# Causal attention in ten steps a group: two narrow key tiles share a step

## The chip, the cores and the metric

The kernel runs on one core of a Trainium2 chip. Inside the core five engines work from instruction queues of their own: TensorE (PE in the rows, with its weight loads as PEld), VectorE (DVE), ScalarE (ACT), GpSimd (POOL) and SyncE (SP, which only issues DMAs here). Each engine runs its instructions in the order in which they are written, and they meet at semaphores. The metric is the device time of one launch in microseconds; lower is better.

## The reference

A layer norm, latent attention with 16 heads over 8 sequences of 1024 tokens, a residual, then a second layer norm and an FP4 feed-forward block. The part that the change touches is the attention proper:

```python
scores = jnp.einsum('bhqd,bhkd->bhqk', Q, K)          # Q, K: 32 plain + 16 rotary features a head
scores = jnp.clip(scores, -80.0, 80.0)
causal = jnp.tril(jnp.ones((S, S), dtype=bool))
scores = jnp.where(causal, scores, -jnp.inf)
weights = jax.nn.softmax(scores / jnp.sqrt(jnp.float32(d_qk)), axis=-1)
attn = jnp.einsum('bhqk,bhkd->bhqd', weights, V)
```

The kernel takes the exponential first and clips afterwards (exp is monotone, so the clip moves to the bounds P_MIN and P_MAX); masked entries become 0 by a bound of 0; the sum over keys (the denominator) is divided out later.

## The kernel before

The program has three stages: projections (until about 350 us), attention (about 350 to 1272 us), feed-forward (to the end). Attention handles 32 **groups**, each one sequence and four heads. Two groups make one turn of a loop: the **even** one (`s == 0`) and the **odd** one (`s == 1`).

Within a group, the 1024 queries are two halves of 512. A **step** is one key tile of 128 keys against the queries of one half that may see it. Half 0 has key tiles 0 to 3, which see 512, 384, 256 and 128 queries; half 1 has key tiles 0 to 7, of which 0 to 4 see 512 queries, and 5, 6, 7 see 384, 256 and 128. So there are NS = 12 steps, numbered k = 0 to 11. A step goes through four operations:

- `score` (PE, L1256): five rounds of matmuls for four heads, keys against queries, into two of three score tiles in PSUM (RING2 = 3; a tile holds two heads).
- `exponentials` (ACT, L1043): two activations, one for each tile (heads 0 and 1, then 2 and 3), from PSUM into one of six `probs` buffers (PROBS = 6; two of the six lie in `r_out`, so the trace shows them as sb_r_out).
- `clip` (DVE, L1121): the 128 columns on the diagonal are clipped against the mask `bound` (L1129), all other columns by L1137. Both take the four heads in one instruction.
- `weigh` (PE, L1276): the probabilities times V, into `ps_o`.

The denominators (`denominators`, L1290) are matmuls with ones into `ps_d`. Eight steps get their own. The four steps k = 4 to 7 (half 1, tiles 0 to 3) are first added up by DVE (`add_up` L1140, four instructions; `add_sums` L1151, two), and one denominator called TOTAL takes their sum.

PE writes, in pass k of its loop: `score` of step k+1, `weigh` of step k-1, then the denominators due. `DENOMS_AT` says at which pass a denominator stands; the last ones of a group and TOTAL (`DENOMS_NEXT`) stand in pass 0 of the next group, behind its `score(1)` and the last `weigh`. ACT and DVE go the same way: in pass k first the exponentials or the clip of step k+1, then what else is due. That is: on ACT the copies of `ps_o` (`copy_out`, between the two exponentials of a step) and of `ps_d` (`copy_denominators`), the rounding of the next group's keys and queries (`round_raw`, L1036, passes 1 and 2), and in the odd group one multiplication for a piece of FP4 weights (L1106, pass 2). On DVE: the low parts of the next group's keys and queries (`rest_of_raw`, L1160), the additions, and small steps of the FP4 quantisation, which are different ones in the even and in the odd group.

Two waits matter below. `score` of a step may begin when the first exponential of the step before has freed its tile:

```python
pe.wait_ge(sc_free, number * 2 + 2)          # L1267
```

And an exponential may write its `probs` buffer when the step that held it before has been weighed and summed (L1049 to L1062).

Of the kernel before, what the change touches and what calls it, by code (L numbers as in the profile page):

```python
# [26 lines left out]
P = 128  # L27
# [6 lines left out]
NI = 4  # L34
# [105 lines left out]
class Front:  # L140


    def __init__(self, nc, ctx, t):
# [16 lines left out]
        self.bound = sb("bound", [P, P])  # L160
# [43 lines left out]
def projections(nc, t, B, front):  # L204
    with ExitStack() as ctx:
# [188 lines left out]
        def _(pool):  # L394
# [19 lines left out]
            pool.affine_select(out=front.bound[:], in_=front.bound[:], compare_op=ALU.is_ge, fill=0.0, base=0,  # L414
                               pattern=[[1, P]], channel_multiplier=-1).then_inc(front.s_cst, 1)
# [287 lines left out]
STEPS = [(half, j, max(0, P * (j - 4 * half))) for half in range(HALF) for j in range(4 * half + 4)]  # L703
NS = len(STEPS)
LOADS2 = 4 * 16


SUMS = [(4, 5), (6, 7)]

TOTAL_STEP = NS - 1  # L710
WARM_UP = 32
# [117 lines left out]
def attention(nc, t, B, front, ahead):  # L829
    with ExitStack() as ctx:  # L830
# [196 lines left out]
        def _(act):  # L1027
# [15 lines left out]
            def exponentials(it2, s, k, first, between=None):  # L1043
                number = step_no(it2, s, k)
                off = STEPS[k][2]
# [3 lines left out]
                act.wait_ge(pv_done, number + 1)  # L1049
# [3 lines left out]
                if k < PROBS and k - PROBS + NS in DENOMS and not first:  # L1053

                    act.wait_ge(denoms_done, denom_no(*preceding(it2, s), DENOMS.index(k - PROBS + NS) + 1))
# [21 lines left out]
            def copy_out(it2, s, half):  # L1077

                act.wait_ge(pv_done, step_no(it2, s, NS if half else 4) + PROBS)
# [7 lines left out]
            def body(it2, s, first, last):  # L1087
                for k in range(NS):
# [3 lines left out]
                    if k == 4:  # L1092
# [14 lines left out]
                    if last and 7 <= k < 7 + GROUPS:  # L1107
                        if k == 7:
                            act.wait_ge(ahead.s_wo, 16)
                        act.copy(ahead.wo_hi[:, k - 7], ahead.x1[:, k - 7]).then_inc(ahead.s_wo_hi, 1)  # L1110
# [7 lines left out]
        def _(dve):  # L1118
            dve.wait_ge(s_cst, 3)

            def clip(it2, s, k):  # L1121
                number = step_no(it2, s, k)
                half, j, off = STEPS[k]

                dve.wait_ge(sc_free, number * 2 + (2 + RING2))
                if j >= 4 * half:

                    pr = probs(k)[:, :, off:off + P]
                    i = dve.scalar_tensor_tensor(out=pr, in0=pr, scalar=P_MIN,  # L1129
                                                 in1=bound[:].unsqueeze(1).to_broadcast([P, NI, P]),  # L1130
# [1044 lines left out]
```

## Time and profile before

| | us |
|---|---|
| median of 3 runs | 2981.09 |
| lowest, highest | 2980.68, 2983.95 |
| the profiled execution, its own time | 2984.09 |
| span of that execution, first to last instruction | 2982.4 |

A row of the timeline gives the start in us from the beginning of the span, the duration, engine, line, operation, output and input, shape, and how many such instructions are merged (x2); square brackets give idle time before it and who ended it. Where two instructions follow one another without a break, their durations overlap a little, and the distance between their starts says what each costs its engine.

### The profile page before, as it was taken

What the parts mean: (1) busy time and instruction counts of PE and PEld (TensorE: products, weight loads), DVE (VectorE), ACT (ScalarE), POOL (GpSimd) and SP (SyncE); (2) the same over time, 40 slices, a digit from 0 to 9 for tenths busy, and PEclk for the clock granted to TensorE, in tenths of its full rate; (3) what the DMA queues carried; (4) which work ended last, traced back from release to release, by engine and by line L of the source; (5) the groups of instructions that cost most, each with busy time, mean ns of one, the idle gap of its engine ahead of it and who ended that gap; (6) DMA issues with size and microseconds to landing.
All of it is one profiled execution on the core that took longest, in us unless ns stands there. A gap on an engine that the chain in (4) does not pass through costs nothing.

```text
span 2982.4 us, 65378 instructions
## 1 busy us (share of the span) xinstructions
PE 2906.9 (97%) x22500; PEld 2133.0 (72%) x22500; DVE 2677.0 (90%) x4593; ACT 1588.7 (53%) x2331; POOL 579.9 (19%) x620
## 2 busy tenths in 40 slices
PE   7999899999999999979999999999999999999999
PEld 6877644444444444468888888888888888888887
DVE  7999788888988988879999999999999999999997
ACT  5666578778777777743333333333333333333333
POOL 3444300000000000012222222222222222222221
PEclk9999999999999999989999999999999999999999
DMA  7889956566565565542222221222222222222220
GB/s 241 283 287 300 290 132 142 135 152 134 138 149 136 138 148 136 140 130 56 59 61 61 60 60 56 53 60 57 60 61 60 60 57 57 55 59 58 60 58 30
DMA packets 335143, 333.27 MB, mean 112 GB/s; under 512 B 60368, under 2 KB 242512, under 8 KB 335056
## 3 DMA queue, kind: packets, MB, share of 16 engines
q1 hardware_dynamic: 335056, 332.26, 40.8%
q8 instruction: 36, 0.59, 0.1%
q14 instruction: 51, 0.42, 0.0%
HBM read 215.52 MB, written 116.65 MB: 111 GB/s over the span
## 4 chain that ended last, share of the span: by engine, by line
PE 55%; DVE 1%; ACT 0%; issue 0%; POOL 0%; DVEq 0%
PE p_ring L2048 20%; PE p_ring L2074 16%; PE ps_od L2048 12%; PE ps_od L2028 6%; PE p_ring L2062 1%; PE ps_od L2074 0%; PE p_ring L2090 0%; PE p_ring L2028 0%; PE p_ring L2055 0%; DVE sb_wg_lo L1936 0%; DVE sb_x_amax L106 0%; DVE sb_stage L1892 0%; POOL sb_stage L1664 0%; DVE sb_xq L120 0%; ACT sb_wg_hi L1753 0%
## 5 line engine op out<-in xcount | busy, mean ns | idle before, releaser
L1065 ACT ACTIVATE sb_probs<-scores 128x1024 f32<-128x1024 f32 (+3 forms) x512 | 405.7, 839 | 112.1 <-PE scores L1271 105.4
L1664 POOL TENSOR_TENSOR sb_stage<-sb_stage,sb_h_inv 128x512 f32<-128x512 f32 (+1 forms) x192 | 190.4, 992 | 857.7 <-DVE sb_h_inv L112 857.7
L2048 PE MATMUL p_ring<-sb_wg_hi,sb_xq_hi 128*128 128x512 f32 (+1 forms) x1024 | 294.9, 369 | 1.8 <-DVE sb_xq_lo L1920 1.1
L2048 PE MATMUL p_ring<-sb_wg_lo,sb_xq_hi 128*128 128x512 f32 (+1 forms) x1024 | 290.6, 365 | 0.0
L2048 PE MATMUL p_ring<-sb_wg_hi,sb_xq_lo 128*128 128x512 f32 (+1 forms) x1024 | 289.4, 364 | 0.0
L2074 PE MATMUL p_ring<-sb_wd_hi,sb_ht_hi 128*128 128x512 f32 x693 | 275.0, 397 | 0.0
L1271 PEld LDWEIGHTS scores<-sb_q_hi,sb_k_hi 32*128 32x128 f32 x1536 | 73.5, 181 | 280.3 <-ACT sb_probs L1065 156.1
L813 POOL TENSOR_TENSOR sb_at_in<-sb_at_in,sb_inv_in 128x512 f32<-128x512 f32 x64 | 95.0, 1485 | 909.1 <-DMA sb_inv_in<-dinv 908.8
L2074 PE MATMUL p_ring<-sb_wd_hi,sb_ht_lo 128*128 128x512 f32 x693 | 270.0, 390 | 0.0
L2074 PE MATMUL p_ring<-sb_wd_lo,sb_ht_hi 128*128 128x512 f32 x693 | 270.0, 390 | 0.0
L1738 ACT ACTIVATE sb_stage<-sb_stage,sb_code_zero 128x512 uint8<-128x512 f32 (+1 forms) x192 | 139.7, 728 | 239.3 <-DVE sb_stage L122 239.3
L1065 ACT ACTIVATE sb_r_out<-scores 128x1024 f32<-128x1024 f32 (+2 forms) x256 | 184.6, 762 | 89.2 <-PE scores L1271 89.2
L1286 PE MATMUL ps_od<-sb_probs,sb_v 128*32 128x512 f32 (+3 forms) x2048 | 225.5, 512 | 0.0
L2048 PEld LDWEIGHTS p_ring<-sb_wg_hi,sb_xq_lo 128*128 128x128 f32 x1024 | 189.1, 188 | 21.8
L2048 PEld LDWEIGHTS p_ring<-sb_wg_lo,sb_xq_hi 128*128 128x128 f32 x1024 | 188.5, 188 | 21.4
L2048 PEld LDWEIGHTS p_ring<-sb_wg_hi,sb_xq_hi 128*128 128x128 f32 x1024 | 185.1, 188 | 22.5 <-issue 2.3
L1137 DVE TENSOR_SCALAR sb_probs<-sb_probs 128x1536 f32<-128x1536 f32 (+3 forms) x224 | 196.6, 877 | 3.9 <-ACT sb_probs L1065 3.9
L1716 ACT ACTIVATE sb_stage<-sb_stage 128x512 f32<-128x512 f32 (+1 forms) x192 | 114.3, 595 | 145.5 <-POOL sb_stage L1664 140.1
L120 DVE SCALAR_TENSOR_TENSOR sb_stage<-sb_stage 128x512 f32<-128x512 f32 (+1 forms) x192 | 184.2, 960 | 6.6
L1271 PE MATMUL scores<-sb_q_hi,sb_k_hi 32*128 32x512 f32 (+3 forms) x1536 | 172.3, 438 | 15.1 <-ACT sb_probs L1065 7.1
L1137 DVE TENSOR_SCALAR sb_r_out<-sb_r_out 128x2048 f32<-128x2048 f32 (+1 forms) x96 | 92.0, 959 | 95.8 <-ACT sb_r_out L1065 95.8
L2048 PE MATMUL ps_od<-sb_wg_hi,sb_xq_hi 128*128 128x512 f32 (+1 forms) x512 | 164.4, 402 | 0.0
(216 smaller groups left out, 7193.9 us busy)
## 6 DMA issues: line engine op xcount, KB each, us to landing
kq<-sb_kq_out SPq DMA_DIRECT2D x32, 1024.0 KB, 7.1
sb_kq_raw<-kq SPq DMA_DIRECT2D x64, 512.0 KB, 7.0
sb_xin<-in_L_attn_x_dram SPq DMA_DIRECT2D x32, 512.0 KB, 7.2
v<-sb_v_out SPq DMA_DIRECT2D x64, 256.0 KB, 6.5
rq<-sb_r_out SPq DMA_DIRECT2D x64, 256.0 KB, 4.5
sb_qr<-rq SPq DMA_DIRECT2D x32, 512.0 KB
sb_kr_hi<-kr SPq DMA_DIRECT2D x32, 512.0 KB
sb_kr_lo<-kr SPq DMA_DIRECT2D x32, 512.0 KB
```

Of the source, the lines that this page charges most:

```text
L120: dve.scalar_tensor_tensor(out=tmp, in0=big, scalar=1.5, in1=y, op0=ALU.max, op1=ALU.add).then_inc(sem, 1)
L813: pool.tensor_tensor(at, at, self.inv_in[:], ALU.mult).then_inc(self.at_divided, 1)
L1065: act.activation(probs(k)[:, 2 * pair:2 * pair + 2, off:BANK], scores[(2 * k + pair) % RING2][:, :, off:BANK], ACT.Exp, scale=SCALE).then_ ...
L1137: i = dve.tensor_scalar(pr, pr, P_MAX, P_MIN, ALU.min, ALU.max)
L1271: mm = pe.matmul(scores[(2 * k + i // 2) % RING2][:, i % 2, off:BANK], key[s][rows, keys], query[s][rows, queries], start=(n == 0), stop=( ...
L1286: mm = pe.matmul(ps_o[rows, off:BANK], v_sb[s][:, j, rows], probs(k)[:, i, off:BANK], start=(j == 0), stop=last)
L1664: pool.tensor_tensor(x, x, spread(h_inv[:, a // QB:b // QB], (b - a) // QB), ALU.mult).then_inc(h_y, 1)
L1716: act.mul(h_big[:, h_slot(r, s), 0:b - a], h[:, a:b], MAGIC).then_inc(h_magic, 1)
L1738: act.activation(out, codes, ACT.Identity, bias=code_zero[:], scale=CODE_STEP).then_inc(h_coded, 1)
L2028: i = pe.matmul(ps[:, 0, :], at[a][:, g, :], wo[b][:, g, :], start=(g == 0 and a == b == 0), stop=(g == GROUPS - 1 and a == 1))
L2048: i = pe.matmul(ps[:, m, 0:b0 - a0], xt[a][:, c, :], wg[b][:, m, c, a0:b0], start=(c == 0 and a == b == 0), stop=(c == DC - 1 and a == 1))
L2074: i = pe.matmul(ps[:, 0, :], ht[a][:, c, :], wd[b][:, c, :], start=(c == 0 and a == b == 0), stop=(c == FC - 1 and a == 1))
```

## The change

The key tile that sees 384 queries and the one that sees 128 fill 512 columns together. They now share a step. The 128 queries of the narrow tile lie in columns 0 to 127, the 384 of the other in columns 128 to 511; both diagonals are then in columns 0 to 255, and the mask is written twice, side by side. A half ends with this pair and then the tile that sees 256. NS is 10: steps 0 to 2 are half 0 (512, pair, 256), steps 3 to 9 half 1 (five of 512, pair, 256).

```diff
-STEPS = [(half, j, max(0, P * (j - 4 * half))) for half in range(HALF) for j in range(4 * half + 4)]
+PAIR = ((1, P, P), (3, 3 * P, 0))
+
+
+def parts_of(half):
+
+    whole = [((j, 0, 0),) for j in range(4 * half + 1)]
+    pair = tuple((4 * half + d, off, at) for d, off, at in PAIR)
+    return whole + [pair, ((4 * half + 2, 2 * P, 2 * P),)]
+
+
+STEPS = [(half, parts) for half in range(HALF) for parts in parts_of(half)]
...
-SUMS = [(4, 5), (6, 7)]
+SUMS = [(3, 4), (5, 6)]
...
-DENOMS = [0, 1, 2, 3, 8, 9, 10, 11, TOTAL]
-DENOMS_AT = {3: [0], 4: [1], 5: [2], 6: [3], 9: [8], 11: [9]}
-DENOMS_NEXT = [10, 11, TOTAL]
-DENOMS_HALF = 4
-DENOM_STEP = 6
+DENOMS = [0, 1, 2, 7, 8, 9, TOTAL]
+DENOMS_AT = {3: [0], 4: [1], 5: [2], 8: [7]}
+DENOMS_NEXT = [8, 9, TOTAL]
+DENOMS_HALF = 3
+DENOM_STEP = 5
```

The wait of an exponential for its buffer follows the new numbers: the buffers of steps 0 to 3 were last used by steps 6 to 9 of the group before, four steps back instead of six. Step 6 is one of those that are added up. And a group now takes 20 score tiles, which is no multiple of three, so `score(0)` meets tiles that step 9 of the group before has just used:

```diff
-                act.wait_ge(pv_done, number + 1)
+                earlier = k - PROBS if k >= PROBS else k + PROBS - NS if k + PROBS < NS else k - NS
+                act.wait_ge(pv_done, number + (earlier - k + PROBS + 1))
...
-                    if k - PROBS + NS in x and not first:
+                    if k < PROBS and earlier + NS in x and not first:
...
-                pe.wait_ge(sc_free, number * 2 + 2)
+                pe.wait_ge(sc_free, number * 2 + (3 if k == 0 else 2))
```

On PE, `score`, `weigh` and `denominators` go over the parts of a step, one after the other; matmuls and columns are as many as before. The clip of a pair is two instructions instead of three, the mask clip over 256 columns:

```diff
+                masked = [at for j, q, at in parts if j >= 4 * half]
+                rest = off + P * len(masked)
+                if masked:
+                    pr = probs(k)[:, :, off:rest]
+                    mask = bound[:, 0:rest - off].unsqueeze(1).to_broadcast([P, NI, rest - off])
+                    i = dve.scalar_tensor_tensor(out=pr, in0=pr, scalar=P_MIN, in1=mask, op0=ALU.max, op1=ALU.min)
+                if rest < BANK:
```

What DVE does behind the clips moves to earlier passes; passes 10 and 11 are gone:

```diff
                     elif k == 4:
                         if not last:
                             rest_of_raw(*following(it2, s), 1)
+                        add_up(it2, s, 0, 0, first)
                     elif k == 5:
-                        add_up(it2, s, 0, 0, first)
+                        add_up(it2, s, 0, 1, first)
+                        if s == 1:
+                            own(dve, w_rounded, rounded + 1)
+                            dve.scalar_tensor_tensor(out=w_tmp[:], in0=w_big[:], scalar=1.5, in1=w_sb[:], op0=ALU.max,
+                                                     op1=ALU.add).then_inc(w_rounded, 1)
                     elif k == 6:
-                        add_up(it2, s, 0, 1, first)
+                        add_up(it2, s, 1, 0, first)
                     elif k == 7:
-                        add_up(it2, s, 1, 0, first)
+                        add_up(it2, s, 1, 1, first)
+                        if s == 1:
+                            own(dve, w_rounded, rounded + 2)
+                            dve.scalar_tensor_tensor(out=w_sb[:], in0=w_big[:], scalar=1.5, in1=w_tmp[:], op0=ALU.max,
+                                                     op1=ALU.subtract, reverse1=True).then_inc(w_rounded, 1)
                     elif k == 8:
-                        add_up(it2, s, 1, 1, first)
-                    elif k == 9:
                         add_sums(it2, s, 0)
...
-                    elif k == 10:
+                    elif k == 9:
                         add_sums(it2, s, 1)
```

The last FP4 multiplication of each group (old pass 11) stands behind `add_sums` of pass 9. ACT keeps `round_raw` in passes 1 and 2 and the FP4 multiplication in pass 2; `copy_out` of half 0 goes from pass 4 to pass 3. At the start GpSimd writes the mask twice, and PE runs 36 warm-up matmuls instead of 32. In the last group, ACT's and DVE's rounding of W_O moves forward by two passes.

On DVE, near the end of the odd group (the loop's second group), before:

```order
L1148 TENSOR_TENSOR sb_v_out<-sb_probs 128x1024
L1125 ISA
L1129 SCALAR_TENSOR_TENSOR sb_probs<-sb_probs,sb_bound 128x4x128
L1137 TENSOR_SCALAR sb_probs<-sb_probs 128x4x256
L1148 TENSOR_TENSOR sb_v_out<-sb_probs 128x1024
L1125 ISA
L1129 SCALAR_TENSOR_TENSOR sb_r_out<-sb_r_out,sb_bound 128x4x128
L1137 TENSOR_SCALAR sb_r_out<-sb_r_out 128x4x128
L59 REGISTER_ALU
L1155 TENSOR_TENSOR sb_v_out<-sb_v_out 128x1024
L819 RECIPROCAL sb_chunk<-sb_chunk 128x64
L1125 ISA
```

and of the change, at the same place:

```order
L1151 SCALAR_TENSOR_TENSOR sb_probs<-sb_probs,sb_bound 128x4x256
L1154 TENSOR_SCALAR sb_probs<-sb_probs 128x4x256
L1165 TENSOR_TENSOR sb_v_out<-sb_r_out,sb_probs 128x1024
L59 REGISTER_ALU
L1238 SCALAR_TENSOR_TENSOR sb_piece_y<-sb_piece_big,sb_piece_tmp 128x528
L1144 ISA
L1151 SCALAR_TENSOR_TENSOR sb_probs<-sb_probs,sb_bound 128x4x128
L1154 TENSOR_SCALAR sb_probs<-sb_probs 128x4x128
L59 REGISTER_ALU
L1172 TENSOR_TENSOR sb_v_out<-sb_v_out 128x1024
L837 RECIPROCAL sb_chunk<-sb_chunk 128x64
L1144 ISA
```

The last `add_up` (the second row of L1148 before, L1165 now) now stands behind the clip of the pair, one clip before the group's last instead of two, and the FP4 rounding of L1209 (now L1238) has moved from behind both `add_sums` to in front of both.

On ACT, in passes 1 to 3 of the odd group, before (sb_k_hi0 and sb_q_hi0 are the rounded keys and queries of the next group, sb_piece_big is the FP4 piece):

```order
L1036 CAST sb_k_hi0<-sb_kq_raw 128x1024
L1049 REGISTER_ALU
L1055 REGISTER_ALU
L1064 ISA
L1065 ACTIVATE sb_probs<-scores0 128x2x128
L1064 REGISTER_ALU
L1065 ACTIVATE sb_probs<-scores1 128x2x128
L1036 CAST sb_q_hi0<-sb_kq_raw 128x1024
L1106 ACTIVATE sb_piece_big<-sb_piece_y 128x528
```

and of the change:

```order
L1054 CAST sb_k_hi0<-sb_kq_raw 128x1024
L1074 REGISTER_ALU
L1083 ISA
L1084 ACTIVATE sb_probs<-scores0 128x1024
L1083 REGISTER_ALU
L1084 ACTIVATE sb_probs<-scores1 128x1024
L1054 CAST sb_q_hi0<-sb_kq_raw 128x1024
L1125 ACTIVATE sb_piece_big<-sb_piece_y 128x528
L1083 ISA
L1084 ACTIVATE sb_r_out<-scores2 128x1024
L1098 REGISTER_ALU
L1100 COPY sb_o<-ps_od 128x512
```

Between the two casts the exponentials are now those of a step with 512 columns, where they were those of the step with 128.

## Rows read from the trace of the kernel before

**Rows 1.** Stretch of 300 us in attention: busy us of each engine, clock.

```profile
core 0: us, PE busy (x) PEld busy (x) DVE busy (x) ACT busy (x) POOL busy (x), PEclk, DMA share, GB/s
900.00:1200.00 300.00, 297.61 (x4336) 145.58 (x4337) 259.23 (x327) 236.87 (x327) 0.00 (x0) 1.00 0.60 141
```

**Rows 2.** Timeline of PE: scores of two groups, then an even group's begin.

```profile
672.57 0.45 PE L1271 MATMUL scores<-sb_q_hi,sb_k_hi 32*128 32x384 f32 x4
...
700.84 0.45 PE L1271 MATMUL scores<-sb_q_hi,sb_k_hi 32*128 32x384 f32 x4
...
701.92 0.42 PE L1286 MATMUL ps_od<-sb_r_out,sb_v 128*32 128x128 f32 x8
702.16 0.83 PE L1305 MATMUL ps_od<-sb_r_out,sb_ones 128*32 128x256 f32 x16
702.81 1.04 PE L1305 MATMUL ps_od<-sb_v_out,sb_ones 128*32 128x512 f32 x8
703.78 0.39 PE L1271 MATMUL scores<-sb_q_hi,sb_k_hi 32*128 32x256 f32 x4
...
704.57 1.06 PE L1286 MATMUL ps_od<-sb_probs,sb_v 128*32 128x512 f32 x8
705.57 0.33 PE L1271 MATMUL scores<-sb_q_hi,sb_k_hi 32*128 32x128 f32 x4
705.73 0.28 PE L1271 MATMUL scores<-sb_q_hi,sb_k_lo 32*128 32x128 f32 x4
...
706.28 0.85 PE L1286 MATMUL ps_od<-sb_probs,sb_v 128*32 128x384 f32 x8
707.06 0.50 PE L1271 MATMUL scores<-sb_q_hi,sb_k_hi 32*128 32x512 f32 x4
```

**Rows 3.** Timeline of PE, the same even group, three passes on.

```profile
708.41 0.64 PE L1286 MATMUL ps_od<-sb_probs,sb_v 128*32 128x256 f32 x8
708.87 1.04 PE L1305 MATMUL ps_od<-sb_probs,sb_ones 128*32 128x512 f32 x8
709.84 0.50 PE L1271 MATMUL scores<-sb_q_hi,sb_k_hi 32*128 32x512 f32 x4
...
711.20 0.43 PE L1286 MATMUL ps_od<-sb_probs,sb_v 128*32 128x128 f32 x8
711.44 0.83 PE L1305 MATMUL ps_od<-sb_probs,sb_ones 128*32 128x384 f32 x8
712.39 0.50 PE L1271 MATMUL scores<-sb_q_hi,sb_k_hi 32*128 32x512 f32 x4
```

**Rows 4.** Timeline of ACT: pass 2 of the odd group, pass 4 of the even.

```profile
678.85 1.07 ACT L1036 CAST sb_q_hi<-sb_kq_raw 128x1024 fp32r<-128x1024 f32 x1
679.78 0.67 ACT L1106 ACTIVATE sb_piece_big<-sb_piece_y 128x528 f32<-128x528 f32 x1
680.33 1.96 ACT L1065 ACTIVATE sb_r_out<-scores 128x1024 f32<-128x1024 f32 x2
...
711.31 1.02 ACT L1065 ACTIVATE sb_r_out<-scores 128x1024 f32<-128x1024 f32 x1 [0.85 <-PE scores L1271]
712.24 0.58 ACT L1081 COPY sb_o<-ps_od 128x512 f32<-128x512 f32 x1
712.70 1.04 ACT L1065 ACTIVATE sb_r_out<-scores 128x1024 f32<-128x1024 f32 x1
```

**Rows 5.** Timeline of DVE: the odd group's second half and its end.

```profile
683.46 1.22 DVE L1160 TENSOR_TENSOR sb_k_lo<-sb_kq_raw,sb_k_hi 128x1024 fp32r<-128x1024 f32 x1
684.59 0.43 DVE L1191 TENSOR_SCALAR sb_piece_big<-sb_piece_big 128x528 int32<-128x528 int32 x1
685.50 1.23 DVE L1137 TENSOR_SCALAR sb_r_out<-sb_r_out 128x2048 f32<-128x2048 f32 x1 [0.48 <-ACT sb_r_out L1065]
...
702.10 0.70 DVE L1209 SCALAR_TENSOR_TENSOR sb_piece_y<-sb_piece_big,sb_piece_tmp 128x528 f32<-128x528 f32 x1
702.72 0.68 DVE L1129 SCALAR_TENSOR_TENSOR sb_probs<-sb_probs,sb_bound 128x512 f32<-128x512 f32 x1
703.33 0.95 DVE L1137 TENSOR_SCALAR sb_probs<-sb_probs 128x1536 f32<-128x1536 f32 x1
```

More of the change, by code:

```diff
@@ L1196, in body @@
                                           ALU.max).then_inc(w_scaled, 1)
-                    elif k == 4 and s == 1:
-                        if not last:
-                            rest_of_raw(*following(it2, s), 1)
-                        own(dve, w_rounded, rounded + 1)
-                        dve.scalar_tensor_tensor(out=w_tmp[:], in0=w_big[:], scalar=1.5, in1=w_sb[:], op0=ALU.max,
-                                                 op1=ALU.add).then_inc(w_rounded, 1)
                     elif k == 2 and s == 0:
@@ L1262, in score @@
                     pe.wait_ge(raw_split, it2 * 4 + (s * 2 + 2 + 2))
[L1263 to L1264 removed]
                 rounds = [(k_hi, q_hi), (k_lo, q_hi), (k_hi, q_lo), (kr_hi, qr), (kr_lo, qr)]
[L1267 to L1268 removed]
+                pe.wait_ge(sc_free, number * 2 + (3 if k == 0 else 2))
+                for j, off, at in parts:
+                    keys = slice(j * P, (j + 1) * P)
+                    queries = slice(half * BANK + off, (half + 1) * BANK)
+                    for n, (key, query) in enumerate(rounds):
+                        for i in range(NI):
+                            rows = slice(DH * i, DH * i + DH)
+                            mm = pe.matmul(scores[(2 * k + i // 2) % RING2][:, i % 2, at:at + BANK - off],
+                                           key[s][rows, keys], query[s][rows, queries], start=(n == 0),
+                                           stop=(n == len(rounds) - 1))
+                            if j == parts[-1][0] and n == len(rounds) - 1 and i % 2 == 1:
+                                mm.then_inc(sc_ready, 1)
@@ L1269, in score, with weigh @@
+            def weigh(it2, s, k):
+                number = step_no(it2, s, k)
+                half, parts = STEPS[k]
+                pe.wait_ge(clipped, number + 1)
+                if parts[0][0] == 0:
+                    pe.wait_ge(o_free, half_no(it2, s, half) + 1)
+                last = parts[0][0] == 4 * half + 2
+                for j, off, at in parts:
                     for i in range(NI):
                         rows = slice(DH * i, DH * i + DH)
-                        mm = pe.matmul(scores[(2 * k + i // 2) % RING2][:, i % 2, off:BANK], key[s][rows, keys],
-                                       query[s][rows, queries], start=(n == 0), stop=(n == len(rounds) - 1))
@@ L1273, in score @@
-                        if n == len(rounds) - 1 and i % 2 == 1:
-                            mm.then_inc(sc_ready, 1)
-            def weigh(it2, s, k):
-                number = step_no(it2, s, k)
-                half, j, off = STEPS[k]
-                pe.wait_ge(clipped, number + 1)
-                if j == 0:
-                    pe.wait_ge(o_free, half_no(it2, s, half) + 1)
-                last = j == 4 * half + 3
-                for i in range(NI):
-                    rows = slice(DH * i, DH * i + DH)
-                    mm = pe.matmul(ps_o[rows, off:BANK], v_sb[s][:, j, rows], probs(k)[:, i, off:BANK],
-                                   start=(j == 0), stop=last)
+                        mm = pe.matmul(ps_o[rows, off:BANK], v_sb[s][:, j, rows], probs(k)[:, i, at:at + BANK - off],
+                                       start=(j == 0), stop=last)
@@ L1303, in denominators @@
                     pe.wait_ge(d_free, half_no(it2, s, half) + 1)
-                for i in range(NI):
-                    mm = pe.matmul(ps_d[DH * i:DH * i + DH, off:BANK], ones[:], src[:, i, off:BANK], start=start,
-                                   stop=n in (DENOMS_HALF - 1, len(DENOMS) - 1))
+                for j, off, at in parts:
+                    for i in range(NI):
+                        mm = pe.matmul(ps_d[DH * i:DH * i + DH, off:BANK], ones[:], src[:, i, at:at + BANK - off],
+                                       start=start, stop=n in (DENOMS_HALF - 1, len(DENOMS) - 1))
                 mm.then_inc(denoms_done, 1)
```

79 lines of the change are left out of this document (34 added, 45 removed).

## The prediction

> **What bounds the kernel now.** Look first at the busy times by stretch. In the middle of attention PE is busy 297.6 of 300 us at the full clock (1.00, its 2.4 GHz level), DVE 259.2, ACT 236.9 [rows 1]. So PE sets the time, but DVE has only 14% to spare. Then read PE's timeline. The second score of a group begins at 672.57, and the next group's at 700.84: a group takes 28.27 us, 32 groups some 905 us [rows 2].
>
> Distances between starts give the price of each block. A score costs 1.35 us at 512 queries (707.06 to 708.41), 1.08 at 384, 0.79 at 256 and 0.71 at 128 [rows 2, 3]. Weights and denominators cost 0.24 for 128 columns, 0.46 for 256, 0.97 to 1.00 for 512 with the way back to a score, 0.78 for 384 with it: about 0.21 for each 128 columns and some 0.12 for the way back [rows 2, 3]. PE is not quite without gaps. From 711.20, where a 512 score has ended, to 712.39, where the next begins, 1.19 us pass, and the two blocks in between need 1.00. There PE waits for the first exponential [rows 3], since the next score needs its tile. I call this the **1.19 rule**: behind a score of 512 the next begins 1.19 us after its end at the earliest. The exponential begins 0.11 after the score's end (711.20 to 711.31) [rows 3, 4].
>
> Last, look at how DVE stands at a group's end. The second `add_sums` ends 0.09 after the start of the instruction behind it, at 702.19 [rows 5]. TOTAL begins at 702.81 [rows 2]. That slack of 0.62 us is all that DVE has there in the odd group; the chain of DVE instructions before it has no gap from 685.50 on [rows 5].
>
> **The change on PE.** Columns and matmuls stay. What goes is, for each of the two pairs of a group, one way back to a score and the slow first round of the narrow score. The pair's score I take at 1.63: 1.08 for 384, and 0.55 for the narrow tile without its first round (705.73 to 706.28) [rows 2]. It can't be over 1.79, the two apart. Below 1.63 I know no row: the rounds of 128 stand 0.11 apart, twice what they would by the columns of the wide ones.
>
> Now one group, t = 0 at its `score(0)`, each term score plus what stands behind it until the next score:
> - score 0: 1.35 + weigh pair 1.00 = 2.35, by the 1.19 rule 2.54
> - score 1, pair: 1.63 + weigh 0.46 + denominators of pair 0.85 and of 256 0.43 + TOTAL 0.97 = 4.34; TOTAL is due at 5.91
> - score 2: 0.79 + 1.00 = 1.79
> - score 3: 2.54 by the rule
> - score 4: 1.35 + 0.46 + 0.97 = 2.78
> - score 5: 1.35 + 0.88 + 0.97 = 3.20
> - score 6: 1.35 + 0.88 + 0.55 = 2.78
> - score 7: 2.54 by the rule
> - score 8, pair: 1.63 + 1.19 = 2.82
> - score 9: 0.79 + 0.88 + 0.97 = 2.64
>
> The sum is 27.97, against 28.27: 0.30 less. Four gaps of 0.19 stay where two were, since a pair's denominators come in one block and leave more passes without one. The new wait of `score(0)` for both exponentials of step 9 costs nothing: 1.85 us of PE work stand behind `score(9)`, and two exponentials of 256 columns are done sooner.
>
> **What ACT does to it.** Pass 2 now holds two exponentials of 512 columns (1.83 us) where two of 128 stood, then the cast of the queries (0.93, 678.85 to 679.78) and in the odd group the FP4 multiplication (0.55) [rows 4]. `score(3)` ends at t = 2.54+4.34+1.79+1.35 = 10.02. ACT begins step 3 at 10.13, is through at 11.96, has cast at 12.89 and multiplied at 13.44. `score(4)` ends at 12.56, so its exponential would like to begin at 12.67. In the even group it begins at 12.89, and `score(5)` may follow 1.08 later, at 13.97; PE comes at 13.99. Nothing is lost. In the odd group it begins at 13.44, and `score(5)` at 14.52: **0.53 us late**. Before, the narrow exponentials covered this work. If that delay weren't there, the odd group would be 0.53 shorter, but see below.
>
> **What DVE does to it.** TOTAL waits for `add_sums`, and this now stands behind the clip of the next group's step 0. In the *even* group's end: exponentials of step 0 begin at 1.46 and end at 3.42 (1.96 for two [rows 4]); clip 0.61 + 0.86; `add_sums` 1.12 and 0.09 until it is seen: 6.10. PE is there at 5.91 and waits **0.19**.
>
> The *odd* group's end is the term that decides. DVE must do, from the clip of step 4 to the last `add_sums`, a chain in which each instruction is ready to go when the one before ends. Its length: the like chain of before, from the clip of step 5 at 685.50 to 702.10, is 16.60 us [rows 5]. The new one begins one full clip earlier in the list and has in addition `rest_of_raw` of the keys 1.13, the FP4 mask step 0.34, the second FP4 rounding 0.62 (702.10 to 702.72), the clip of step 0 1.47 (702.72, and 703.33 with 0.95 less 0.09) and the clip of the pair [rows 5]. The clip of 384 (1.19) and that of 128 (0.61) are out. For the pair's clip the trace has no row. Its mask part is 1024 elements with two inputs; the two-input instruction of 1024 costs 1.13, twice the mask clip of 512 costs 1.22. Could it run at double speed, 0.61 would do; nothing in the rows of two inputs hints at it. I take 1.13, plus 0.58 for the rest (by the slope between 1536 and 2048 elements). So 16.60 + 1.13 + 0.34 + 0.62 + 1.47 + 1.71 - 1.80 = 20.07.
>
> It can't start before both exponentials of step 4, between which `copy_out` now stands: 13.44 + 0.19 + 0.93 + 0.46 + 1.04 = 16.06 [rows 4]. It ends at 36.13, seen at 36.22. The odd group itself takes 27.97 + 0.53 + 0.19 = 28.69 and TOTAL is due 5.91 later, at 34.60. PE waits **1.62 us** in all: some 0.4 at `score(1)`, because the exponential of step 0 waits for the last `add_up` (its buffer held step 6), the rest at TOTAL. Queued behind TOTAL are `score(2)` and all that follows. DVE catches up in the next group's first passes, so the even group begins clean but late.
>
> **A rule weighed.** By the rows, joining two instructions of DVE saves 0.09. The Trainium skill (VectorE: DVE Perf Modes, "The TRN2 errata — SBUF-src ops pay a fixed extra latency per instruction") says that a large tile pays the fixed cost once, many small ones each time; on its figure of 151 cycles at 0.96 GHz joining would save 0.16, over 64 pairs 10 us of DVE. By that rule alone the kernel gets faster; here the saving doesn't reach the chain, which is longer for other reasons.
>
> **The sum.** Two groups: 28.69 + 27.97 + 1.62 = 58.28, before 56.54: 1.74 more, over 16 turns 27.8. The very first group has no late DVE before it: less 1.6. The work of GpSimd on the second mask lies beside the projections, the four warm-up matmuls beside loads. In the last group DVE's list is about as long (no `rest_of_raw`, four roundings of W_O instead). Total +26.2 us. The profiled execution of 2984.09 us would become 3010.3; it stood 3.0 above the median 2981.09, so the forecast for the median is **3007**.
>
> **Rivals.**
> - *DVE isn't late, ACT is.* If the chain were done when TOTAL is due, only the 0.53 stay: 27.97 + 28.50 = 56.47 for two groups, 1 us less in all: 2980, no change. For it: DVE is idle 14% of the time [rows 1], and instructions may overlap more than I count. Against it: 1.6 us in 20 is a wide miss for distances read from the same chain.
> - *The other side: ACT and DVE shed fixed costs, and PE's path rules.* The place is the odd group's end; it decides for faster if the chain takes 18.4 us or less, and ACT's multiplication is hidden. Then 2 x 27.97 = 55.94, 0.60 less, over 16 turns 9.6: 2971. This is what the page's rule would give. For it: the kernel is bound by PE now [rows 1]. Against it: the slack of 0.62 us at TOTAL [rows 2, 5] is less than one moved clip.
> - *The mask clip of the pair runs at double speed.* The chain is 0.52 shorter, the wait 1.1: 8 us less than forecast, 2999. Slower still.
> - *PE's clock.* Should the granted clock fall to its 1.2 GHz level for one score behind each long wait, 16 x 1.35 = 22 us more: 3029. The row shows 1.00 throughout attention [rows 1], with short waits only.
>
> **How the numbers follow.** The forecast has 0.62 (3007, its own bounds 2996 to 3018 from 0.1 us an engine and group, and the costs left open), double speed 0.10, no change 0.10, faster 0.12, the clock 0.06. The range takes in all but the last two: 2976 to 3020. Measured differences below 0.2% (6 us) can't be told from none. Slower by more than that 0.78, within 0.10, faster 0.12.
>
> **What would show it.** In the profile of the changed kernel: PE idle before the TOTAL that stands in every even group (of the odd group before it), released by `add_sums`, 1 to 1.3 us, and some 0.2 before the one in an odd group. ACT idle before the exponential of step 0, released by the last `add_up`, behind the odd group. Periods that alternate, about 28.7 and 29.6. The pair's score 1.63, its mask clip 1.22 long. DVE without a gap from the clip of step 4 to TOTAL. The forecast is wrong if DVE shows gaps there, if the period is the same for both groups, or if waits appear at `weigh` (a clip that comes late) or at `score(0)`, where I count none.

## The result and the profile after

The changed kernel takes 3061.3 us (four runs, 3060.51 to 3062.12), the kernel before 2981.6. The ratio is 1.0266, its 95% interval 1.0248 to 1.0284. The forecast was 3007, with a range up to 3020. The sign was right; the time is 54 us off, outside the range. So the first question is where those 54 us are, and a difference of two totals can't say it. Two landmarks in PE's timeline can: the first score of attention and the first transposes of the feed-forward stage.

| us | before | after | difference | forecast |
|---|---|---|---|---|
| start of attention | 352.6 | 352.9 | 0.3 | 0 |
| attention, to the first feed-forward transposes | 921.9 | 946.6 | **24.7** | 26.2 |
| feed-forward, to the end of the span | 1707.9 | 1759.4 | **51.5** | 0 |

Attention did about what the prediction says. Two thirds of the loss lie in a stage that the change doesn't touch.

**Attention after.** The same stretch as [rows 1], in the changed kernel:

```profile
900.00:1200.00 300.00, 284.58 (x4192) 143.50 (x4188) 251.86 (x298) 223.72 (x273) 0.00 (x0) 1.00 0.56 139
```

PE is busy 284.6 of 300 us where it was 297.6. The group periods alternate, 28.85 and 29.7. The place that decides is the one of [rows 2], the `score` of the pair and the denominators behind it, here at the end of an odd group (PE's timeline):

```profile
704.55 1.07 PE L1302 MATMUL ps_od<-sb_probs,sb_v 128*32 128x384 f32 x16
706.25 0.46 PE L1285 MATMUL scores<-sb_q_hi,sb_k_hi 32*128 32x384 f32 x4 [0.63 <-ACT sb_probs L1084]
...
707.23 0.25 PE L1285 MATMUL scores<-sb_q_hi,sb_k_hi 32*128 32x128 f32 x4
...
707.85 0.64 PE L1302 MATMUL ps_od<-sb_probs,sb_v 128*32 128x256 f32 x8
708.31 1.48 PE L1322 MATMUL ps_od<-sb_probs,sb_ones 128*32 128x384 f32 x24
710.81 1.07 PE L1322 MATMUL ps_od<-sb_v_out,sb_ones 128*32 128x512 f32 x8 [1.02 <-DVE sb_v_out L1172]
```

Two waits, in the brackets of the second and the last row: `score(1)` waits for the exponential of step 0, and TOTAL for the second `add_sums`. The first is ACT's, who itself waits for the last `add_up` (ACT's timeline):

```profile
705.17 1.94 ACT L1084 ACTIVATE sb_probs<-scores 128x1024 f32<-128x1024 f32 x2 [2.65 <-DVE sb_v_out L1165]
```

Both lead to DVE, which in the same stretch works without a gap (DVE's timeline, same kernel):

```profile
690.58 1.23 DVE L1154 TENSOR_SCALAR sb_r_out<-sb_r_out 128x2048 f32<-128x2048 f32 x1 [2.56 <-ACT sb_r_out L1084]
...
702.10 1.22 DVE L1151 SCALAR_TENSOR_TENSOR sb_probs<-sb_probs,sb_bound 128x1024 f32<-128x1024 f32 x1
703.24 0.69 DVE L1154 TENSOR_SCALAR sb_probs<-sb_probs 128x1024 f32<-128x1024 f32 x1
703.84 1.22 DVE L1165 TENSOR_TENSOR sb_v_out<-sb_r_out,sb_probs 128x1024 f32<-128x1024 f32 x1
704.97 0.70 DVE L1238 SCALAR_TENSOR_TENSOR sb_piece_y<-sb_piece_big,sb_piece_tmp 128x528 f32<-128x528 f32 x1
...
707.66 0.55 DVE L837 RECIPROCAL sb_chunk<-sb_chunk 128x64 f32<-128x64 f32 x1
...
709.53 1.22 DVE L1172 TENSOR_TENSOR sb_v_out<-sb_v_out 128x1024 f32<-128x1024 f32 x1
```

From the clip of step 4 at 690.58 to the second `add_sums` at 709.53 there is no idle bracket; the mask clip of the pair costs 1.14 (702.10 to 703.24), forecast 1.13.

**Feed-forward after.** Now the stretch that nobody had touched, before and after:

```profile
1400.00:2900.00 1500.00, 1500.00 (x7020) 1271.79 (x7019) 1405.45 (x2785) 579.63 (x930) 392.05 (x464) 1.00 0.21 58
```

```profile
1400.00:2900.00 1500.00, 1463.53 (x6775) 1234.06 (x6774) 1357.97 (x2687) 559.28 (x896) 378.19 (x448) 0.99 0.21 57
```

PE now idles 36 us of the 1500, and all engines have done less. Before, each tile of 128 rows takes 25.86 us. After, the loop (four tiles a turn) has one tile in each turn that takes some 3 us longer, and in every second turn the next one takes longer too: 29.38, 25.96, 25.92, 25.88, 29.71, 27.45. The view of waits of this stretch names waits that before does not have:

```profile
PEld p_ring L2072 <- issue: 40.2, 13, 3.6
PE p_ring L2072 <- ACT sb_x_codes L1743: 36.5, 13, 3.3
DVE sb_x L1867 <- issue: 26.9, 13, 2.3
DVE sb_moments L1872 <- issue: 18.2, 13, 1.8
```

The numbers are us in total, times, longest. "issue" is time in which the engine waited for nothing that the profile shows. The loop makes 14 turns and so jumps back 13 times; DVE stops 13 times at one place, for 1.9 to 2.3 us, and 13 times at a second, for 1.1 to 1.8. On DVE's timeline:

```profile
1652.94 0.68 DVE L1948 TENSOR_TENSOR sb_x<-p_ring,sb_x 128x512 f32<-128x512 f32 x1
1655.73 0.69 DVE L1867 TENSOR_TENSOR sb_x<-ps_od,sb_x 128x512 f32<-128x512 f32 x1 [2.10 <-issue]
1656.45 0.70 DVE L1869 BATCH_NORM_STATS2 sb_stats<-sb_x 128x6 f32<-128x512 f32 x1
1658.93 0.18 DVE L1872 BATCH_NORM_AGGREGATE sb_moments<-sb_stats 128x2 f32<-128x6 f32 x1 [1.78 <-issue]
```

L1948 ends the loop's body and L1867 begins it. The second stop lies in front of the seventh instruction of the body (the semaphore step at L1871, behind two computing instructions and the waits and register steps between them).

Part of the loss comes by way of PE's clock. Once a turn PE waits out DVE's stops, for 2.3 to 3.3 us. In every second turn, six times in all, the clock granted behind that wait is at its 1.2 GHz level for 3.4 us. PE's timeline at one such place, and the busy row of these 3.4 us (0.50 is the granted clock):

```profile
1886.63 0.30 PE L2072 MATMUL p_ring<-sb_ident,sb_x_codes 128*128 128x128 f32 x1 [3.15 <-ACT sb_x_codes L1743]
```

```profile
1886.90:1890.30 3.40, 3.40 (x9) 2.72 (x9) 3.26 (x9) 1.69 (x4) 0.09 (x1) 0.50 0.00 0
```

The matmuls there begin 0.43 us apart instead of 0.23, and the tile takes 27.45 instead of 25.9. Six times 1.6 us makes some 10 of the 51.5.

One more view has changed, the DMA queue that carries the engines' own instructions (packets, MB). First before, then after, the same 1500 us:

```profile
q14 instruction: 36, 0.29, 0.1%
```

```profile
q14 instruction: 97, 0.79, 0.2%
```

61 packets of 8 KB more, four to five for each jump back. That looks as if DVE fetched its loop's code again in every turn and stood still meanwhile; the experiments test it. Before, 36 packets pass without any stop of DVE, and the view doesn't say which engine they are for.

### The profile page after: what moved, and what is told of

The parts are those of the page before. It is cut to its first block, busy times and chain, and to the rows that moved or that the text cites. A ratio compares the mean times of both kernels' runs of the same rounds, so it can differ in the third digit from the quotient of the medians.

```text
span 3058.9 us, 64803 instructions
## 1 busy us (share of the span) xinstructions
PE 2913.0 (95%) x22508; PEld 2150.2 (70%) x22508; DVE 2672.4 (87%) x4529; ACT 1576.1 (52%) x2203; POOL 579.1 (19%) x621
## 4 chain that ended last, share of the span: by engine, by line
issue 26%; PE 13%; DVE 10%; POOL 6%; ACT 1%; POOLq 0%; DMA 0%; SPq 0%; DVEq 0%; ACTq 0%
PE p_ring L2091 4%; PE p_ring L2065 4%; PE ps_od L2065 2%; POOL sb_at_lo L1667 2%; POOL sb_at_in L831 2%; POOL sb_stage L1681 1%; DVE sb_x_amax L106 1%; PE ps_od L2045 1%; DVE sb_stage L120 1%; DVE sb_xq L120 1%; POOL sb_rstd L1673 1%; DVE sb_stage L1909 1%; DVE sb_stage L118 1%; DVE sb_x_big L118 1%; DVE sb_h_inv L110 1%
## 5 line engine op out<-in xcount | busy, mean ns | idle before, releaser
L1084 ACT ACTIVATE sb_probs<-scores 128x1024 f32<-128x1024 f32 (+1 forms) x512 | 446.3, 918 | 199.9 <-PE scores L1285 156.5
L1154 DVE TENSOR_SCALAR sb_probs<-sb_probs 128x1536 f32<-128x1536 f32 (+3 forms) x256 | 210.3, 821 | 67.3 <-ACT sb_probs L1084 67.3
L1302 PE MATMUL ps_od<-sb_probs,sb_v 128*32 128x512 f32 (+3 forms) x2560 | 246.2, 475 | 2.8 <-DVE sb_probs L1154 2.8
L1285 PE MATMUL scores<-sb_q_hi,sb_k_hi 32*128 32x512 f32 (+3 forms) x1536 | 166.0, 421 | 33.6 <-ACT sb_probs L1084 15.6
L1151 DVE SCALAR_TENSOR_TENSOR sb_probs<-sb_probs,sb_bound 128x512 f32<-128x512 f32 (+1 forms) x192 | 165.6, 862 | 22.0 <-ACT sb_probs L1084 19.5
L1322 PE MATMUL ps_od<-sb_probs,sb_ones 128*32 128x512 f32 (+3 forms) x2048 | 168.4, 435 | 0.0
```

Source lines behind the costliest of these rows:

```text
L1084: act.activation(probs(k)[:, 2 * pair:2 * pair + 2, off:BANK], scores[(2 * k + pair) % RING2][:, :, off:BANK], ACT.Exp, scale=SCALE).then_ ...
L1151: i = dve.scalar_tensor_tensor(out=pr, in0=pr, scalar=P_MIN, in1=mask, op0=ALU.max, op1=ALU.min)
L1154: i = dve.tensor_scalar(pr, pr, P_MAX, P_MIN, ALU.min, ALU.max)
L1285: mm = pe.matmul(scores[(2 * k + i // 2) % RING2][:, i % 2, at:at + BANK - off], key[s][rows, keys], query[s][rows, queries], start=(n == ...
L1302: mm = pe.matmul(ps_o[rows, off:BANK], v_sb[s][:, j, rows], probs(k)[:, i, at:at + BANK - off], start=(j == 0), stop=last)
L1322: mm = pe.matmul(ps_d[DH * i:DH * i + DH, off:BANK], ones[:], src[:, i, at:at + BANK - off], start=start, stop=n in (DENOMS_HALF - 1, len( ...
```

## The experiments

Positions below are those of DVE's instructions in the compiled program, waits included. The feed-forward loop of DVE has 341. Before, it stands at 720 to 1061; the change makes attention's DVE code 16 instructions shorter, so after it stands at 704 to 1045. All of DVE's code behind a point can be moved by waits on a semaphore that has long reached its value; two such waits make one instruction. They stand ahead of the projections' normalisation:

```diff
             dve.sem_inc(stored[1], STORES1)
+            for _ in range(32):
+                dve.wait_ge(piece_stored, 16)
```

| kernel | DVE's loop | us | ratio to before, 95% | feed-forward, us | packets in all |
|---|---|---|---|---|---|
| before | 720 to 1061 | 2981 | | 1707.9 | 51 |
| after | 704 to 1045 | 3061.3 | 1.0248 to 1.0284 | 1759.4 | 116 |
| after_moved8 | 712 to 1053 | 3007.3 | 1.0067 to 1.0101 | 1707.2 | 51 |
| after_moved16 | 720 to 1061 | 3008.8 | 1.0071 to 1.0105 | 1707.4 | 51 |
| before_moved176 | 896 to 1237 | 3026.6 | 1.0134 to 1.0168 | 1738.9 | 117 |
| before_moved256 | 976 to 1317 | 3003.4 | 1.0051 to 1.0085 | 1706.6 | 53 |

### The position of the code

**after_moved16** has the 32 waits above, **before_moved176** 352 of them in the kernel before.

> The changed kernel with 16 more instructions on VectorE, satisfied waits at the very start of the program, while VectorE waits for its first input. That puts VectorE's feed-forward loop back to where it stood in the kernel before (it begins 16 instructions earlier in the changed one). Theory 'fetch': the 51 us that the untouched feed-forward stage lost come from the place of that loop in VectorE's program, which now spans one block more than is kept loaded; then the loop turns of 107 us become 103.4 again, the stage is 51 us shorter, and the kernel takes about 3010 us, 28 above the kernel before. Rival 'state': attention leaves something behind (a late transfer, a semaphore, the clock) that slows the feed-forward stage; then it stays at 3061 us.

> The kernel before with 176 more instructions on VectorE at the very start, nothing else. Theory 'fetch': its feed-forward loop of 341 instructions is pushed so far that its end crosses the next block, the same stalls appear, and the kernel takes 2982 + 51 = 3033 us, with two idle stretches put down to issue on VectorE in each turn of four tiles. Rival 'state': 2982 to 2990 us, for the waits themselves only.

Moving the code by 16 instructions, with nothing else, gives back 52 us: 3008.8. Moving it in the kernel before, whose attention nobody changed, costs 45 us. Of these 12.9 lie ahead of attention, which begins at 365.5 instead of 352.6: that is the price of the waits themselves, and it should have been in the expectation. 31 lie in the feed-forward stage, 20 less than was expected from the changed kernel. The waits view of 1400 to 2900 us of before_moved176 has the first of the two stops, at the same place of the body, and not the second:

```profile
PEld p_ring L2058 <- issue: 27.1, 13, 2.5
DVE sb_x L1853 <- issue: 25.6, 13, 2.4
PE p_ring L2058 <- ACT sb_x_codes L1729: 23.4, 13, 2.2
```

PE's wait is shorter too (23.4 us in all, 36.5 in the changed kernel), and the clock falls to its 1.2 GHz level once inside the loop instead of six times.

> The kernel before, with 512 waits on VectorE on a semaphore that has long reached its value, ahead of the normalisation of the projections: they make 256 instructions, all of VectorE's code behind them moves by 256, and the feed-forward loop stands at instructions 976 to 1317 instead of 720 to 1061. Nothing is left out. Theory (what counts is how many blocks of 256 instructions the loop touches, and the block edges repeat every 256): this is the kernel before again, feed-forward tiles of 25.86 us, some 51 packets in the queue of the instructions or a few more, 2981 to 2984 with the extra waits. Rival (a loop further down in the program is dearer, or the extra waits themselves were what made before_moved176 slow): at least before_moved176's 3026, with tiles of 27.5 to 28 us in between.

> The changed kernel with VectorE's code moved by 8 instructions instead of 16: its feed-forward loop stands at 712 to 1053 (after: 704 to 1045, slow; after_moved16: 720 to 1061, not slow). Nothing is left out. Theory (one edge of a block lies between 704 and 720, and the loop is either cut by it or not): the time is one of the two, 3061 or 3009, and nothing between; which one says on which side of 712 the edge lies. Rival (the cost grows with the number of instructions beyond the edge): about 3035.

The feed-forward stage of **before_moved256** is that of before: 1706.6 us, tiles of 25.83 to 25.92, 53 packets. Its total missed the expectation by 20 us because 512 waits aren't free. The first 100 us show it; first this kernel, then before:

```profile
0.00:100.00 100.00, 61.51 (x283) 51.08 (x284) 59.63 (x106) 45.85 (x62) 24.21 (x26) 1.00 0.56 189
```

```profile
0.00:100.00 100.00, 82.19 (x385) 68.33 (x386) 80.74 (x144) 59.70 (x80) 34.01 (x33) 0.98 0.74 249
```

PE has done 21 us less by then, and attention begins at 374.8: 22.2 us for 256 instructions of two waits. The rival (further down is dearer) falls. **after_moved8** is at 3007.3, at the good level and not between the levels. All positions fit one picture: an edge between 704 and 712, and one every 256 instructions from there. The four positions without a loss (712, 720, 976 and the 736 of the kernels below) then have the loop of 341 instructions in two blocks, the two with a loss in three (704 to 1045 begins up to eight instructions ahead of an edge; 896 to 1237 ends 13 to 21 behind one). The Trainium skill (Runtime: NRT & Kernel Launch, "Instruction fetch mechanics") states just this: an instruction memory of 32 KiB for most engines, filled in 16 KiB blocks of 256 instructions, so that it holds two of them, and a taken branch out of that window must fetch before it goes on. The six positions agree with the 256 and with the two; the packets in the trace are 8 KB each.

The two kinds of overhang differ by 20 us. In both DVE stops at the jump back. In the changed kernel it stops a second time six instructions further on, where the picture has the edge; in before_moved176 the next edge is far behind the jump, and there is no second stop. With the second stop PE waits 13 us more, and with the longer waits come five more falls of the clock, some 8 us. The instruction packets are as many in both, 97 in the 1500 us. So the second stop would be no further fetch, but one that DVE is upon at once and has to wait out; that is read from its place, and no run tried it.

### Which work holds the odd group's end

All kernels from here have 64 waits (loop at 736 to 1077), so that only attention differs; the feed-forward stage took 1704 to 1708 us in each. They are compared with after_moved16. **no_fp4_in_chain** leaves out three FP4 instructions on DVE in the odd group: the exponent mask and both roundings.

> The changed kernel, with VectorE's program moved (feed-forward loop 32 instructions later), and three FP4 instructions of the odd group left out of VectorE's list (the exponent mask and both roundings; the weights of these pieces are then not rounded). They cost 0.34 + 0.62 + 0.62 = 1.58 us between the clip of step 4 and the last add_sums. Theory 'VectorE's chain sets TOTAL': the period of the following even group falls from 29.7 to 28.2, 16 x 1.5 = 24 us less than after_moved16, 2986 us if that takes 3010. Rival 'the exponentials set it' (the narrow exponentials no longer cover the casts): under 5 us less, since VectorE would only idle longer.

2988.6, so 20.3 less where 24 was expected; the odd end's period falls from 29.74 to 28.47. So the wait at TOTAL is set by what stands in DVE's list.

**magic_later** moves ACT's FP4 multiplication to pass 4, and the mask step that needs it on DVE behind the first `add_up`:

```diff
-                    if k == 2 and s == 1:
+                    if k == 4 and s == 1:
                         act.wait_ge(w_y, it2 + 1)
                         act.mul(w_big[:], w_sb[:], MAGIC).then_inc(w_magic, 1)
```

> As after_moved16 (VectorE's loops lie where they cost nothing), and of the odd group ACT's FP4 multiplication stands in the pass of step 4 instead of step 2, with its mask step on DVE behind the first add_up. Nothing is left out. Theory (two delays that don't overlap: score(5) is 0.51 us late because of this multiplication, TOTAL 1.2 late because of DVE's list): the 0.51 goes, DVE's chain starts 0.51 sooner and keeps its length, so the wait at TOTAL stays: 16 x 0.51 = 8 us less than after_moved16's 3008.8, so 3000.5. Rival (DVE's chain does not depend on the exponential of step 4 but on its own total load, so that what PE gains there it waits for at TOTAL): 3007 to 3009, with the wait before TOTAL 0.5 longer.

2999.4: 9.4 less, forecast 8. The rival asked for longer waits at TOTAL, and they did not grow. The waits views of attention (480 to 1220 us), first after_moved16, then magic_later, show the wait for sb_r_out, that of `score(5)`, gone and the others unchanged:

```profile
PE ps_od L1325 <- DVE sb_v_out L1175: 12.5, 12, 1.0
PE scores L1288 <- ACT sb_probs L1087: 7.5, 12, 0.6
PE scores L1288 <- ACT sb_r_out L1087: 5.8, 13, 0.4
```

```profile
PE ps_od L1326 <- DVE sb_v_out L1175: 12.4, 12, 1.0
PE scores L1289 <- ACT sb_probs L1087: 7.3, 12, 0.6
```

**raw_in_gaps** has the same change and also moves `rest_of_raw` from passes 3 and 4 to 1 and 2.

> The changed kernel, moved as above, with all work kept but in another order. VectorE takes the low parts of the next group's keys and queries in passes 1 and 2, where it waits for exponentials of step 3 and 4, instead of passes 3 and 4; ScalarE does the FP4 multiplication of the odd group in pass 4 instead of 2, and VectorE its exponent mask behind it. Theory 'chain': 2.27 us leave the chain, which was 1.62 too long, and the late exponential of step 4 (0.53) goes: two groups take 27.97 x 2 + 0.19 = 56.1 us against 58.6, 16 x 2.4 = 39 us less than after_moved16, about 2971 us, faster than the kernel before. Rival 'throughput': VectorE has no real slack and the wait comes back elsewhere; then two groups stay above 57 us and the kernel above 2985.

2989.7, a miss by 19, and where the rival had it: above 2985, with 57.4 us for two groups. The wait at `score(1)` went, but not that at TOTAL:

```profile
703.60 0.64 PE L1323 MATMUL ps_od<-sb_v_out,sb_ones 128*32 128x512 f32 x4 [0.88 <-DVE sb_v_out L1175]
```

The chain was no longer one chain. Its last part starts when the exponentials of the pair of step 8 are done (the second ends at 694.85), however early DVE is, and is too long by itself (DVE's timeline, same kernel):

```profile
694.88 1.23 DVE L1154 SCALAR_TENSOR_TENSOR sb_probs<-sb_probs,sb_bound 128x1024 f32<-128x1024 f32 x1
...
697.76 0.70 DVE L1237 SCALAR_TENSOR_TENSOR sb_piece_y<-sb_piece_big,sb_piece_tmp 128x528 f32<-128x528 f32 x1
...
700.46 0.54 DVE L840 RECIPROCAL sb_chunk<-sb_chunk 128x64 f32<-128x64 f32 x1
...
702.33 1.22 DVE L1175 TENSOR_TENSOR sb_v_out<-sb_v_out 128x1024 f32<-128x1024 f32 x1
```

From 694.88 to 703.5 it is 8.6 us; PE would have been at TOTAL some 0.9 sooner. Of the 8.6, 0.62 are an FP4 rounding and 0.46 a reciprocal that nobody waits for. **short_tail** puts these two behind the last `add_sums`.

> As raw_in_gaps (2989.7 us; its wait before TOTAL at the odd group's end was 1.08 us), and the second FP4 rounding (0.62) and the reciprocal of the chunk (0.46) stand behind the last add_sums instead of between the adds. Nothing is left out. Theory (what lies on DVE between the clip of step 8's pair and add_sums decides, whatever its sort): the wait falls from 1.08 to about 0.3, 16 x 0.77 = 12 us less: 2977.5; at least to 0.45: 2980. Rival (the add_sums wait for the exponentials of the next step 0, not for DVE's other work): no change, 2988 to 2990. Against before (2981.3) the theory gives about no change.

2980.0 (ratio to before 0.9986 to 1.0005): 9.7 less, at the upper of the two values given, and both groups now take 28.3. So it was not DVE's load as a whole, the rival of raw_in_gaps: the load is the same here, only its order isn't. What is left is a wait of 0.3 at TOTAL in every group. **total_later** puts TOTAL one pass later:

```diff
+                    if k == 1 and not first:
+                        denominators(*preceding(it2, s), TOTAL)
                     for x in DENOMS_AT.get(k, ()):
```

> As short_tail, and TOTAL stands one pass later on PE (behind the weighing of step 0 instead of before it), with the copy of the denominators on ACT one pass later too. Nothing is left out. Theory (the waits before TOTAL, some 0.3 us at the end of every group, are nothing but TOTAL being due before add_sums is ready): both go, 32 x 0.3 = 9.6 us less than short_tail, 2968 to 2972, which would be faster than both kernels. Rival (DVE's load as a whole, or the copy of the denominators which is now next to the rounding of the keys on ACT, sets the pace): the wait moves to the exponential of the next steps or to a weigh, and the time is short_tail's.

2970.3 (0.9948 to 0.9976). The period is 27.95 to 28.02: this is the 27.97 of the prediction's sum, in which PE waits for nothing but the four gaps of the 1.19 rule. So the waits of 0.3 at TOTAL are gone. The busy row of this kernel:

```profile
900.00:1200.00 300.00, 294.97 (x4376) 151.12 (x4368) 263.21 (x309) 232.50 (x284) 0.00 (x0) 1.00 0.62 145
```

### Filling the gaps of the 1.19 rule

**spread** cuts the denominators into pieces, so that two of the four gaps are filled, those behind `score(3)` and `score(7)`; those behind `score(0)` and the pair's `score(8)` stay:

```diff
+PIECES = [(0, 0, 0, 512), (1, 0, 128, 512), (1, 1, 384, 512), (2, 0, 256, 384), (2, 0, 384, 512),
+          (7, 0, 0, 512), (8, 0, 128, 512), (8, 1, 384, 512), (9, 0, 256, 512), TOTAL]
-DENOMS_AT = {3: [0], 4: [1], 5: [2], 8: [7]}
+DENOMS_AT = {2: [0], 3: [1], 4: [2], 5: [3], 6: [4], 8: [5]}
```

> As total_later, and the denominators of steps 0, 1 and 2 are cut into five blocks and handed out over the passes 2 to 6, so that the passes of 2.35 us behind score(3) and score(7), which the rule stretches to 2.54, are filled; those of step 7 stay where they are. Columns and matmuls of PE stay. Theory (PE's sum of blocks and the 1.19 rule set the period): two gaps of 0.19 go from each group, 32 x 0.38 = 12 us less than total_later, some 2958 to 2960. Rival (DVE is now the bound, at some 24.6 us of 27.5 with its own waits): the two gaps turn into waits for clips, and the time is total_later's within 3 us.

**2961.1 us** (ratio to before 0.9911 to 0.9944), periods 27.60 and 27.66. It is the fastest here, 20 us under before and 100 under after. DVE has become busier, at 267.9 of 300 us (259.2 in [rows 1]), and still PE doesn't wait for it.

```profile
900.00:1200.00 300.00, 297.40 (x4530) 155.79 (x4523) 267.88 (x320) 236.39 (x289) 0.00 (x0) 1.00 0.62 144
```

**before_spread** gives the kernel before the same treatment, as far as its passes allow.

> The kernel before, twelve steps a group, with the denominators of step 2 cut in two: the 128 columns from 256 on stand in the pass behind those of step 1, the rest where they were. Nothing is left out, and VectorE's code is where it was. This asks what joining the tiles is worth by itself, once a like spreading of the denominators is given to both kernels (spread, with ten steps, has 2961). Of the two gaps of 0.19 us that the 1.19 rule leaves in a group of before, this can fill one, since the passes around the other have nothing to give. Theory (PE's blocks and the 1.19 rule set the period, and the ten steps are worth what they save on PE, 0.3 us a group before gaps): period 28.08, 32 x 0.19 = 6 us less than before: 2975 to 2977, so that some 15 us of spread's gain need the ten steps. Rival (the gain of spread came from the spreading and not from the ten steps): 2965 or less.

2977.5 (0.9975 to 0.9994), period 28.13. One gap of 0.19 was to go and 0.14 went. 16 us remain between it and spread. The new order of DVE's and ACT's work has little to give with twelve steps, where PE is busy 297.6 of 300 us [rows 1] as it is. Were both gaps filled, 28.27 less 0.38 would be 27.89 us (an estimate from the rows), against 27.63 in spread. So at least 8 of the 16 us need the ten steps; the other 8 need them too if the second gap can't be filled with twelve, which no run tried.

## Why the prediction failed, and where it held

**What failed is the sum's total: a term put at nothing without a reason.** "Total +26.2 us" counts 16 turns of attention and takes the feed-forward stage at 0, without a word on it. Its code is the same, but it stands at another place. The missing term is 51.5 us, some 4 for each of the 13 jumps back of DVE's loop: DVE's two stops, and behind them six stretches of PE's clock at its lower level, some 10 of the 51.5. after_moved8 and after_moved16 take it away (1707 us) with the code of attention unchanged; their totals, 3007.3 and 3008.8, are what the forecast of 3007 priced. None of the rivals held this case, and so the range ended at 3020. The difference of instruction counts could have been read from the program before any run: 16 fewer on DVE, in front of a loop of 341.

**The change on PE: held.** The forecast of the passes, with the measured distances behind it (the passes with a wait from short_tail or total_later): score 0 2.54, 2.55; scores 1 and 2 together 6.13, 6.11; score 3 2.54, 2.54; score 4 2.78, 2.80; score 5 3.20, 3.22; score 6 2.78, 2.80; score 7 2.54, 2.55; score 8 2.82, 2.79; score 9 2.64, 2.65. The pair's score is 1.60 us (706.25 to 707.85), taken at 1.63. Sum 27.97, and 27.99 in total_later.

**What ACT does: held.** Forecast 0.53 late at `score(5)` of the odd group; its pass took 3.31 instead of 2.80, so 0.51. PE's timeline of the changed kernel:

```profile
747.76 0.51 PE L1285 MATMUL scores<-sb_q_hi,sb_k_hi 32*128 32x512 f32 x4 [0.44 <-ACT sb_r_out L1084]
```

magic_later took just this away.

**What DVE does: held, each wait about 0.1 larger.** Odd group's end: forecast 1.62, of which some 0.4 at `score(1)`; measured 0.51 there and 1.21 at TOTAL, 1.72. Even group's end: 0.19, measured 0.30. The pair of groups takes 58.57, forecast 58.28, before 56.54. The chain of 20.07 us is in the trace 20.1: from 690.58 to the end of `add_sums` at 710.67. But the argument treated it as one piece of which every part counts alike. That is true of the changed kernel and stops being true as soon as something is taken out, as raw_in_gaps showed: then the last 8.6 us stand alone.

**The sum for attention: near, in part by luck.** 30 periods cost 29.3 us more (878.4 against 849.1 from the second group's begin to the last's), where the forecast has some 26. The last group and what follows cost 0.7. The very first group took 28.9 us instead of 34.2, so 5.3 us came back where the prediction had 1.6. Some 3 of them are the clock's and not the order's: over this group the granted clock was 0.90 before and 0.98 after, and PE was busy 27.5 and 24.5 us. In after_moved16 it was 0.95, and the group took 31.6. Together 24.7 against 26.2, and 27.5 in after_moved16.

**A rule weighed.** By the Trainium skill (VectorE: DVE Perf Modes, "The TRN2 errata — SBUF-src ops pay a fixed extra latency per instruction") joining two instructions would save 0.16 us, the prediction's estimate from its 151 cycles. The trace has half of that: the mask clip over 1024 elements took 1.14 us, two of 512 take 0.61 each, so 0.08 is saved. DVE's chain grew as the rows said. The measurement decides against that rival here, and against double speed.

**Rivals.** "ACT only" (2980) and "shed fixed costs" (2971) fall with the waits at TOTAL. The clock stayed at 1.00 in attention from the second group on, behind waits of 1 us too; the fall that this rival feared came in the feed-forward stage, behind waits of 2.6 to 3.3 us, and not behind all of that size. Yet 2971 was reached, by total_later: not because joining shortened DVE's chain, but because work nobody waited for was moved out of it and TOTAL was put where its input is ready.

## What to carry to other kernels

When an edit changes how many instructions stand ahead of a loop, compare the loop's positions too: count the blocks that it touches, and look after the run at the queue of the instructions and at waits on "issue" that come once a turn. Where a stage that nobody touched has changed, time the stages by landmarks before explaining anything in the stage that was. Joining narrow pieces saves the engine that pays for their starts, but it moves the cover that they gave to other engines' side work; put what no one waits for behind the result that someone waits for, and only then judge the join.

## What the hardware showed that was not expected

- A loop of 341 VectorE instructions costs 51 us more in 13 jumps back (4.0 us each) when it begins at instruction 704 of the program instead of 712 or 720, and 31 us more (2.4 each) at 896; at 976 it costs nothing more. The signs are two stops of DVE at each jump, of up to 2.3 and 1.8 us (one stop in the loop at 896), and 97 instead of 36 instruction packets in 1500 us.
- With a wait of PE of 2.3 to 3.3 us in each turn, its clock was at the 1.2 GHz level for 3.4 us behind every second one, which cost 1.6 us each time. With waits of 1.3 to 2.2 us (the loop at 896) that happened once in the loop.
- 256 VectorE instructions at the program's start that hold nothing but two met waits each together delayed attention by 22.2 us, 87 ns an instruction; 176 delayed it by 12.9, 73 ns. Eight to 32 showed no delay.
- A mask clip with two inputs costs 1.14 us for 1024 elements a partition and 0.61 for 512.
